# A Mamba tower on one core: one silu group of ScalarE per step, and a new table of places for everything around the state loop

## The reference, cut to what matters

```
def mamba_block(x, W_in, conv_w, conv_b, W_x, W_dt, b_dt, A_log, Dp, W_out):
    xr = x @ W_in                                  # 256 -> 2 x 512
    x_in, res = jnp.split(xr, 2, axis=-1)
    u = silu(conv of 4 taps over x_in + conv_b)
    dbl = u @ W_x                                  # dt (64), B (16), C (16)
    delta = softplus(dt @ W_dt + b_dt)
    A = -exp(A_log)
    h = exp(d_t * A) * h + (d_t * u_t) * B_t       # over 2048 tokens in all, 16 states, 512 channels
    y = sum over states of h * C_t  + u * Dp
    return (y * silu(res)) @ W_out
```

## Time and profile before

| | |
|---|---|
| median of 3 runs | 1891.31 us (1889.51 to 1893.72) |
| the profiled execution | 1891.32 us, its span 1889.2 us |
| busy, share of the span | PE 94%, PEld 75%, DVE 82%, ACT 82%, POOL 80% |
| mean granted clock of TensorE | 0.984 |
| first scan of step 0; of step 1; of step 13 | 132.6; 226.1; 1365.8 us |
| first scan of step 14; of step 15; the last scan ends | 1461.0; 1563.0; 1676 us |

### The profile page before, as it was taken

One profiled execution on the slowest core, in us unless ns is written; L12 is line 12 of the kernel. 1 busy time (PEld: TensorE's weight loads), 2 busy tenths in 40 slices (PEclk: granted clock), 3 DMA queues, 4 the chain that ended last, 5 costly groups with the idle time before them and its releaser, 6 DMA issues.

```text
span 1889.2 us, 31478 instructions
## 1 busy us (share of the span) xinstructions
PE 1782.5 (94%) x11920; PEld 1415.4 (75%) x11920; DVE 1552.8 (82%) x1707; ACT 1543.8 (82%) x2579; POOL 1510.4 (80%) x874
## 2 busy tenths in 40 slices
PE   6989899999999999999999999999999988789993
PEld 3447687878787878787878787878788777789993
DVE  1368989898989898989898989898989989853243
ACT  0269999999999999999999999999999987832230
POOL 0029999999999999999999999999999987631422
PEclk9999999999999999999999999999999989899997
DMA  7211111121212121211111111111111211163641
GB/s 272 99 68 45 58 47 68 44 71 40 74 38 76 37 71 44 71 44 67 48 62 52 59 56 57 58 54 61 50 65 46 80 57 68 38 250 129 231 143 59
DMA packets 46392, 144.24 MB, mean 76 GB/s; under 512 B 7009, under 2 KB 18529, under 8 KB 42914
## 3 DMA queue, kind: packets, MB, share of 16 engines
q1 hardware_dynamic: 41538, 114.97, 17.5%
q0 software_dynamic: 4704, 27.27, 4.0%
HBM read 119.67 MB, written 22.54 MB: 75 GB/s over the span
## 4 chain that ended last, share of the span: by engine, by line
PE 41%; ACT 24%; POOL 20%; DVE 8%; issue 6%; DMA 1%; SPq 0%; POOLq 0%; DVEq 0%; ACTq 0%
POOL hid L524 13%; ACT hid L709 12%; ACT dub_t L724 9%; PE b_ps L1469 8%; PE y_all L1482 7%; DVE hid L1141 6%; PE bank_a L1601 4%; POOL dub_t L515 4%; PE bank_b L1337 3%; PE y_all L1222 3%; PE bank_a L1337 2%; POOL du L505 2%; PE b_ps L1585 2%; PE y_all L1585 2%; PE bank_a L1346 2%
## 5 line engine op out<-in xcount | busy, mean ns | idle before, releaser
L1141 DVE TENSOR_TENSOR_SCAN hid<-hid,b_ps 128x512 f32<-128x512 f32 x1024 | 1199.2, 1206 | 102.0 <-PE b_ps L1469 89.6
L524 POOL TENSOR_TENSOR hid<-hid,c_rep 128x1024 f32<-128x1024 f32 x506 | 1191.8, 2390 | 97.7 <-DVE hid L1141 97.4
L1469 PEld LDWEIGHTS b_ps<-ident,dub_t 128*128 128x128 f32 x4096 | 486.4, 142 | 300.2 <-issue 180.5
L1469 PE MATMUL b_ps<-ident,dub_t 128*128 128x128 f32 x4096 | 630.7, 277 | 42.7 <-DVE hid L1141 40.4
L709 ACT ACTIVATE hid<-delta,neg_a 128x512 f32<-128x512 f32 x1024 | 659.6, 714 | 0.2
L1482 PE MATMUL y_all<-ident,hid 128*128 128x128 f32 x4096 | 620.5, 275 | 0.0
L724 ACT ACTIVATE dub_t<-du_t,b_t 128x512 f32<-128x512 f32 x784 | 505.2, 714 | 30.0 <-PE b_ps L1469 29.6
L1482 PEld LDWEIGHTS y_all<-ident,hid 128*128 128x128 f32 x4096 | 484.1, 142 | 2.9 <-POOL hid L524 2.7
L515 POOL TENSOR_SCALAR dub_t<-du_t,b_t 128x512 f32<-128x512 f32 x240 | 162.4, 702 | 0.0
L934 DVE SCALAR_TENSOR_TENSOR u<-bank_b,conv_w_sb,u 128x511 f32<-128x511 f32 (+2 forms) x192 | 139.6, 727 | 0.7
L1316 PE MATMUL bank_b<-xn,w_in_sb 128*128 128x512 f32 x256 | 129.9, 603 | 5.4 <-DVE u L934 3.9
(11 more groups left out here) (211 smaller groups left out, 1593.7 us busy)
## 6 DMA issues: line engine op xcount, KB each, us to landing
c_rep<-bc_dram SPq DMA_DIRECT2D x128, 512.0 KB, 3.7
hid<-x_t SPq DMA_DIRECT2D x4, 2048.0 KB, 8.5
xt<-x_dram SPq DMA_DIRECT2D x15, 512.0 KB, 3.4
x_dram<-x_out SPq DMA_DIRECT2D x15, 512.0 KB, 2.9
z_dram<-du SPq DMA_DIRECT2D x2, 1408.0 KB, 19.2
y_dram<-hid SPq DMA_DIRECT2D x22, 128.0 KB, 2.1
h_dram<-hid SPq DMA_DIRECT2D x4, 512.0 KB, 4.3
x_dram<-hid SPq DMA_DIRECT2D x3, 512.0 KB, 2.7
```

What stands on the lines that cost most here:

```text
L524: nc.gpsimd.tensor_tensor(part, part, c_rep[:, n % 2, s % GROUP, :].unsqueeze(1) .broadcast_to([P, HALF, SEQ]), ALU.mult).then_inc(hc_read ...
L1141: nc.vector.tensor_tensor_scan(hid[:, i % RING, d, :], hid[:, i % RING, d, :], b_ps[d % 2][:, :], 0.0, ALU.mult, ALU.add)\
L1469: last = nc.tensor.transpose(b_ps[d % 2][:, c * P:(c + 1) * P], dub_t[:, i % DUB, c, d * P:(d + 1) * P], ident[:, :])
```

## The change

The places of all pieces are changed at once, and with them who empties which bank ahead of whom:

- ACT: before, the silu work of step k+1 stood in two groups in state 4, each with a load of the silu table ahead of it and a load of the exp/ln table behind it (gate 1, u, gate 0; then gates 3 and 2). Now there is one group with two loads: gate 0 behind the decays of state 4, gate 1 in the middle of `times_b(5)`, u behind it, gates 3 and 2 ahead of the decays of state 5.
- POOL makes the products of states 4, 7, 9, 12 instead of 3, 7, 9, 13; its first half of du comes one half later.
- PE: the eight in_r products now stand at slots (1,0) to (4,0), in the order of the gates; to_x and back, du_turn and skip move by one to four slots. squares and spread_norm use bank_a and not bank_b, and squares waits for the copy of dbl (`dbl_ready`).
- DVE: taps and gating move by up to three slots: the first gating from (1,0) to (0,3), the last taps from (15,3), (0,0) and (0,1) of the next step to (15,2), (15,3) and (0,3).

No instruction is added, and two table loads of each step's four are removed. The diff, cut to its core:

```diff
 DVE_C = 13
-POOL_B = (3, 7, 9, 13)
+POOL_B = (4, 7, 9, 12)
...
-            back_bank = (bank_b, bank_a, bank_a, bank_a)
+            back_bank = (bank_b, bank_b, bank_a, bank_a)
...
-                                if live(k + 1) and (s, half) == (7, 0):
+                                if live(k + 1) and (s, half) == (7, 1):
                                     times_u(k + 1, 0)
...
                     def between(k, s, part):
                         at = (s, part)
-                        if at == (0, 4) and live(k):
+                        if at == (0, 0) and live(k):
                             scale_u(k, 0)
-                        if at == (1, 2) and live(k):
+                        if at == (2, 0) and live(k - 2):
+                            x_copy(k - 2, 1)
+                        if at == (3, 0) and live(k):
                             scale_u(k, 1)
-                        if at == (1, 3) and live(k - 2):
-                            x_copy(k - 2, 1)
-                        if at == (4, 1) and live(k + 1):
+                        if at == (4, 2) and live(k + 1):
                             nc.scalar.preload_act_table(ACT.Silu)
+                            gate(k + 1, 0)
+                        if at == (4, 3) and live(k + 1):
                             gate(k + 1, 1)
+                        if at == (4, 4) and live(k + 1):
                             for m in range(NI):
                                 silu(k + 1, m)
-                            gate(k + 1, 0)
-                            nc.scalar.preload_act_table_set("natural_log_exp_and_others")
-                        if at == (4, 2) and live(k + 1):
-                            nc.scalar.preload_act_table(ACT.Silu)
+                        if at == (5, 0) and live(k + 1):
                             gate(k + 1, 3)
-                        if at == (4, 3) and live(k + 1):
                             gate(k + 1, 2)
                             nc.scalar.preload_act_table_set("natural_log_exp_and_others")
                         if at == (5, 1) and live(k + 2):
                             square(k + 2)
-                        if at == (5, 4) and live(k + 1):
+                        if at == (5, 3) and inner(k - 1):
+                            y_copy(k - 1, 0)
+                        if at == (6, 1) and live(k + 1):
                             dbl_copy(k + 1)
-                        if at == (6, 0) and inner(k - 1):
-                            y_copy(k - 1, 0)
-                        if at == (6, 1) and inner(k - 1):
+                        if at == (6, 2) and inner(k - 1):
                             y_copy(k - 1, 1)
                         if at == (7, 2) and live(k + 1):
                             delta_exp(k + 1, 0)
                             delta_log(k + 1, 0)
+                        if at == (7, 3) and live(k):
+                            scale_u(k, 2)
                         if at == (7, 4) and live(k + 1):
                             delta_exp(k + 1, 1)
-                        if at == (8, 0) and live(k + 1):
                             delta_log(k + 1, 1)
+                            delta_exp(k + 1, 2)
                         if at == (8, 1) and live(k + 1):
-                            delta_exp(k + 1, 2)
+                            delta_log(k + 1, 2)
+                        if at == (8, 3) and live(k):
+                            scale_u(k, 3)
                         if at == (8, 3) and live(k + 1):
-                            delta_log(k + 1, 2)
-                        if at == (8, 4) and live(k + 1):
                             delta_exp(k + 1, 3)
-                        if at == (8, 4) and live(k):
-                            scale_u(k, 2)
                         if at == (8, 4) and live(k + 1):
                             delta_log(k + 1, 3)
-                        if at == (9, 3) and inner(k - 1):
+                        if at == (9, 0) and inner(k - 1):
                             y_copy(k - 1, 2)
-                        if at == (10, 1) and inner(k - 1):
+                        if at == (10, 2) and inner(k - 1):
                             y_copy(k - 1, 3)
-                        if at == (10, 2) and live(k):
-                            scale_u(k, 3)
-                        if at == (10, 2) and live(k + 1):
+                        if at == (10, 3) and live(k + 1):
                             du_copy(k + 1, 0)
-                        if at == (10, 4) and live(k + 1):
+                        if at == (11, 0) and live(k + 1):
                             du_copy(k + 1, 1)
-                        if at == (11, 1) and live(k + 1):
+                        if at == (12, 1) and live(k + 1):
                             du_copy(k + 1, 2)
-                        if at == (12, 1) and live(k + 1):
+                        if at == (13, 0) and live(k + 1):
                             du_copy(k + 1, 3)
-                        if at == (15, 3) and inner(k - 1):
+                        if at == (15, 2) and inner(k - 1):
                             x_copy(k - 1, 0)
...
-                        nc.vector.tensor_scalar(norm[:, :], bank_b[:, 0:TC], 1e-24, 1.0 / D,
+                        nc.vector.tensor_scalar(norm[:, :], bank_a[:, 0:TC], 1e-24, 1.0 / D,
...
-                    SOFTPLUS_AT = {0: (6, 3), 1: (7, 2), 2: (8, 0), 3: (8, 1)}
-                    TAP_AT = {(0, 0): (9, 2), (0, 1): (10, 0), (0, 2): (10, 2), (0, 3): (10, 3),
-                              (1, 0): (11, 1), (1, 1): (11, 3), (1, 2): (12, 1), (1, 3): (12, 2),
-                              (2, 0): (13, 1), (2, 1): (13, 2), (2, 2): (13, 3), (2, 3): (14, 1),
-                              (3, 0): (15, 0), (3, 1): (15, 3), (3, 2): (16, 0), (3, 3): (16, 1)}
-                    GATING_AT = {0: (1, 0), 1: (1, 1), 2: (1, 2), 3: (2, 1)}
-                    MEAN_SQUARE_AT, B_COPY_AT, NORMALIZE_AT = (6, 1), (6, 3), (8, 3)
+                    SOFTPLUS_AT = {0: (6, 3), 1: (7, 2), 2: (8, 0), 3: (8, 2)}
+                    TAP_AT = {(0, 0): (9, 2), (0, 1): (9, 3), (0, 2): (10, 1), (0, 3): (10, 3),
+                              (1, 0): (11, 1), (1, 1): (11, 3), (1, 2): (12, 0), (1, 3): (12, 2),
+                              (2, 0): (13, 1), (2, 1): (13, 3), (2, 2): (14, 0), (2, 3): (14, 1),
+                              (3, 0): (15, 0), (3, 1): (15, 2), (3, 2): (15, 3), (3, 3): (16, 3)}
+                    GATING_AT = {0: (0, 3), 1: (1, 2), 2: (1, 3), 3: (2, 1)}
+                    MEAN_SQUARE_AT, B_COPY_AT, NORMALIZE_AT = (6, 0), (6, 3), (8, 3)
...
                     def squares(k):
                         pe.wait_ge(msq_ready, k + 1)
-                        if live(k - 3):
-                            pe.wait_ge(y_ready, NI * (k - 3) + 1)
-                        elif live(k - 1):
-                            pe.wait_ge(gate_ready, TC * (k - 1) + 3)
+                        if live(k - 1):
+                            pe.wait_ge(dbl_ready, k)
                         for t in range(TC):
                             for c in range(DC):
-                                last = nc.tensor.matmul(bank_b[:, t:t + 1], xn[:, c, t * P:(t + 1) * P],
+                                last = nc.tensor.matmul(bank_a[:, t:t + 1], xn[:, c, t * P:(t + 1) * P],
                                                         ones[:, 0:1], start=c == 0, stop=c == DC - 1, skip_group_check=True)
                         last.then_inc(ss_done, 1)
 
                     def spread_norm(k):
                         pe.wait_ge(norm_ready, k + 1)
-                        if live(k - 1):
-                            pe.wait_ge(delta_ready, NI * (k - 1) + 4)
+                        if live(k - 3):
+                            pe.wait_ge(y_ready, NI * (k - 3) + 3)
+                        elif live(k - 1):
+                            pe.wait_ge(delta_ready, NI * (k - 1) + 3)
                         else:
                             pe.wait_ge(ss_ready, k + 1)
                         for t in range(TC):
-                            last = nc.tensor.transpose(bank_b[:, t * P:(t + 1) * P], norm[:, t:t + 1].broadcast_to([P, P]),
+                            last = nc.tensor.transpose(bank_a[:, t * P:(t + 1) * P], norm[:, t:t + 1].broadcast_to([P, P]),
                                                        ident[:, :])
                         last.then_inc(rs_done, 1)
...
                             pe.wait_ge(conv[3], CONV * (k + 1))
                         elif tc == 2:
+                            pe.wait_ge(gate_ready, TC * k + 1)
+                        elif tc == 3:
                             pe.wait_ge(gate_ready, TC * k + 2)
-                        elif tc == 3:
-                            pe.wait_ge(gate_ready, TC * k + 1)
...
                     def b_turn(k):
                         pe.wait_ge(dbl_ready, k + 1)
-                        if live(k + 1):
-                            pe.wait_ge(ss_ready, k + 2)
```

(21 more changed lines are left out.)

32 lines of the change are left out of this document (18 added, 14 removed).

## The result

The changed kernel takes 1894.38 us (median of 19 runs, 1891.21 to 1900.65) against 1891.29 us before: ratio 1.0021, interval 1.0012 to 1.0030. In a second series it was 1892.16 against 1892.72 (1.0006, 0.9996 to 1.0015); ratios and intervals are made of all runs, so they need not be the quotient of two medians. So it is slower by 0 to 0.3%; forecast were 1884.0 and a gain. The profiled execution has a span of 1892.6 us against 1889.2.

What follows compares the result with a forecast made beforehand. PE was taken to bound 29 us of each step, DVE some 65. From 1891.3: steps 1 to 13 5.9 less, step 0 1.0, step 14 2.95, head 2.5 more, so 7.3 less, 1884.0 us; range 1877 to 1893.

Steps and rivals of the forecast that it cites:

- The steps: Steps 1 to 13: 0.45 us less each, between 0 and 0.65, together 5.9 us.
- The rule for a pair: DVE's cost in a stretch: PE's work there plus 2.0 us, minus DVE's own work from two slots earlier.
- the new costliest stretch: Slots (1,0) to (6,3): DVE waits 5.8 us there, 0.5 us less than before.
- the wait of 3.1 us at gate 3: ACT reaches gate 3 3.1 us before in_r (3,1) at slot (4,0); by itself this costs nothing.
- The 0.2 us for the first gating: First gating at (0,3) needs sum_states of (15,0), costing DVE about 0.2 us each step.
- the 0.25 of small waits: DVE's small waits, taps behind products and out_x behind the x copy: 0.25 us less a step.
- PE bounds the stretch: PE's work fills 28.7 of 29.1 us from (2,2) to (7,1); taking time from ACT alone frees 0.1.
- The tie at gate 0: ACT needs 49.1 us to finish gate 0, PE 49.2 to reach in_r (2,0); error 0.3.
- rival 2: ACT comes late to gate 0, at in_r (2,0) in slot (2,3); 1901 us if 1.2 late; chance 0.14.
- The three waits: In the head, to_x waits 1.3 us for gates, squares 0.8 for dbl's copy, to_delta 0.35 longer: +2.5 us.
- The loads do count in part: Step 0: removing two table loads saves 1.0 us, a choice between 0 and 2.57.
- two claims about the first du_turn: Step 14: b_states (10,1) ahead cuts the 1.66 us wait to 0.3; clock stays up; together 2.5 us saved.

Runs made afterwards that it cites:

- four_loads: The changed kernel with the two removed table loads put back, between the silus of u and gate 3: 1893.8 us, ratio to before 1.0007.
- tap_out: The changed kernel with one VectorE tap moved from behind scan (0,3) to behind scan (0,1): 1901.6 us, ratio to before 1.0059.
- less_in_r: The changed kernel without the second in_r product for chunk 3, in all steps but the first: 1890.5 us, ratio to before 0.9990.
- fill_taps: The changed kernel with head holes filled, step 14's layer norm pieces on GpSimd, three head taps at old places: 1885.4 us, ratio to before 0.9968.
- add_on_pool: The changed kernel with VectorE's small 128x4 addition of step 14 given to GpSimd: 1894.7 us, ratio to before 1.0018.
- no_port: The changed kernel with the 128x4 addition and the four scalings of step 14 given to GpSimd: 1886.5 us, ratio to before 0.9975.
- dut_back: no_port with the first du_turn back from slot (10,1) to its old place (10,0): 1889.2 us, ratio to before 0.9991.

## Why the prediction was wrong

- **The steps: right.** Forecast were 0.45 us less for each, 0.36 came (4.7 us for 13 against 5.9). The rule for a pair, the new costliest stretch (5.8 us of waiting; the view shows 4.9 in ten waits from slot (3,0) to (6,3), 5.9 with the prediction's 0.1 for each), the wait of 3.1 us at gate 3 (3.16) and two loads without a drain all stand. The 0.2 us for the first gating did not appear, nor did the 0.25 of small waits, and a wait of 0.4 us for a decay is left at (6,1). That ACT's saving buys nothing is now shown (four_loads); that the place of a DVE piece decides what it costs too (tap_out). "PE bounds the stretch" was too simple: less_in_r shows PE and DVE as one chain with a lead of two slots.
- **The tie at gate 0: right.** The gate waits 0.19 us for the last gating, and in_r for the gate no more than 0.1; rival 2 did not happen, and what made the kernel slower is in none of the rivals.
- **The head: mis-sized.** The three waits were forecast at 1.3, 0.8 and 0.35 and are in the trace with 1.17, 0.78 and 0.35, some 2.8 with each piece's own start. I added them up and stopped. Pieces that come 3 us later also meet TensorE's clock at another point: in_x at the lower level cost 1.7 more, and one more tap now stands ahead of the first scan (0.67; the head of fill_taps, without it, is 0.5 shorter). Together 5.2 instead of 2.5.
- **Step 0: wrong.** "The loads do count in part" gave -1.0. Beside the same short stretch of low clock four_loads, with the loads, has 93.1, and add_on_pool, without them, 93.2: they don't count. What goes with the length of step 0 is a second low stretch: from 140 to 146 us the granted clock is 0.58 after, where before it was back at 1.00 by 138. Profiles of this order with the long stretch have 94.1 us or more, those with the short one 92.7 to 93.3.
- **Step 14: the failed step.** -2.95 was the step's 0.45 and 2.5 for two claims about the first du_turn; measured are +0.6. At that place the forecast came true: the du_turn waits 0.36 us and no fall of the clock follows. That this shortens the step is what failed. The wait of 1.66 us is not saved: POOL is waited for at the next pieces (0.34 and 0.80 us in no_port), and with the old place back (dut_back) the step is as long. The low clock is not saved either: the step's mean is 0.95 before and after, the falls only come later. And a term was put at nothing without a reason that is worth more than both: one DVE instruction of 128x4 that took 3.72 us and now takes 5.64, with TensorE's hole and low clock behind it; without it step 14 takes 96.1 us. Its row stood in the trace of the kernel before. Its length is not its own work (0.17 us alone) but the time to POOL's next gap, and the change moves POOL's work. With it gone from both kernels step 14 is 2.4 us shorter in the new order (98.5 and 96.1), which is near the forecast by luck of the clock, as dut_back's 96.1 with the old place shows.

By parts, against the forecast of -7.3: the head 2.8 more, step 0 1.7, the steps 1.2, step 14 3.6, step 15 0.8 less, and 2.2 by chance at the start, together +3.4 us in the profile. The 2.2 are of one profile and say nothing of the medians; the second series shows less because none of its 11 runs has the lower mean clock of 0.979 or 0.98 that seven of the first 19 have.

What stays open: what makes TensorE's clock fall in one execution and not in another at the same place. In the nine profiles with the new head and its holes the clock fell near 100 us in three (add_on_pool, four_loads, less_in_r), in none of the five without these holes. Seven of the 19 runs of the changed kernel have a mean clock of 0.979 or 0.98 and 1896.6 us or more, the others 0.982 or 0.983 and 1894.8 or less. That fits holes that make a fall more likely; nothing here proves it, and in no_port a hole of 3.3 us in step 14 (TensorE waits for GpSimd's scalings) was followed by no fall.

## What to carry to other kernels

Count what stands once as closely as what stands in the loop: here 13 steps gave 4.7 us, and the head, with three waits and what came of them, took all of it back. An instruction whose duration is many times that of the same instruction elsewhere in the trace is a wait in disguise; find what it waits for before moving the other engine's work, and put both on one engine; a gap by itself passed the stall on to the next such instruction here. A saving on an engine that already waits (two table loads here) is spent as a longer wait, whatever its share of busy time.

## What the runs showed of the hardware

- A TENSOR_SCALAR of VectorE from SBUF to SBUF (128x4, alone 0.17 us) stood still for 5.64 us while GpSimd instructions followed one directly behind the other, and ended within 0.03 us of GpSimd's first gap; a gap of 0.1 us is enough.
- Others of 128x256, with their two scalars from SBUF (alone 0.40 us), took 2.45 and 2.44, each to 0.15 us behind the end of one GpSimd instruction, the first of them though the next had followed directly. BATCH_NORM_STATS2 of 128x256, from SBUF too, kept its 0.4 beside GpSimd.
- The same hole of 1.66 us on TensorE (1.65 in one) was followed by a granted clock of 0.57 over the next four us in one execution and of 1.00 in two others.
- A product of in_x (four records) takes 1.98 us at full clock and 3.68 in the low stretch, so a piece's place in the head can cost more than the waits ahead of it.
